# Attention and low-rank feed-forward on one core: the negated row maxima reach DRAM by a transfer of single elements

## The reference, cut to what matters

```python
q = einsum('bsd,dhk->bshk', LN(x), Wq) + bq          # k and v alike
attn = softmax(einsum('bqhd,bkhd->bhqk', q / 8, k), axis=-1)
att = einsum('bqhd,hdm->bqm', einsum('bhqk,bkhd->bqhd', attn, v), Wo) + bo
x = x + LN(att)
x = x + LN(gelu(LN(x) @ U1 @ V1 + b1) @ U2 @ V2 + b2)
```

## Time and profile before

| what | value |
|---|---|
| median of three runs | 2462.3 us (2461.09 to 2462.98) |
| the profiled execution's own time | 2463.04 us |
| its span, first to last instruction | 2461.0 us |
| mean granted TensorE clock | 0.986 |
| busy: PE, ACT, POOL, DVE | 97%, 88%, 84%, 82% |
| the chain that ended last | PE 88%, POOL 8%, DVE 2% |

### The profile page before, as it was taken

One profiled execution on the slowest core, in us unless ns is written; L12 is line 12 of the kernel. 1 busy time (PEld: TensorE's weight loads), 2 busy tenths in 40 slices (PEclk: granted clock), 3 DMA queues, 4 the chain that ended last, 5 costly groups with the idle time before them and its releaser, 6 DMA issues.

```text
span 2461.0 us, 44224 instructions
## 1 busy us (share of the span) xinstructions
PE 2382.9 (97%) x15724; PEld 1183.9 (48%) x15724; DVE 2011.0 (82%) x3148; ACT 2154.1 (88%) x2499; POOL 2071.8 (84%) x1188
## 2 busy tenths in 40 slices
PE   6999999999999999999999999999999999998985
PEld 3455544545545454545445445445545445544432
DVE  6888888888888888888888888888888888886735
ACT  5998999998999999898999999899999998997873
POOL 4888888888888888888888888888888888898985
PEclk8999999999999999999999999999999999999987
DMA  1000001000010000000010000100001000010001
GB/s 50 28 14 27 27 15 32 27 22 19 27 32 15 27 27 19 28 27 27 14 32 27 18 24 27 33 14 27 27 14 32 27 23 26 27 40 18 23 27 35
DMA packets 60773, 63.13 MB, mean 26 GB/s; under 512 B 25900, under 2 KB 44204, under 8 KB 60556
## 3 DMA queue, kind: packets, MB, share of 16 engines
q1 hardware_dynamic: 59548, 59.97, 7.8%
q10 hardware_dynamic: 1008, 0.33, 0.1%
HBM read 57.40 MB, written 2.62 MB: 24 GB/s over the span
## 4 chain that ended last, share of the span: by engine, by line
PE 88%; POOL 8%; DVE 2%; issue 1%; ACT 1%; DMA 0%; POOLq 0%; ACTq 0%; DVEq 0%
PE o_ps L419 34%; PE spare_ps L376 13%; PE score_ps L398 10%; PE score_ps L404 9%; PE score_ps L401 9%; POOL total L1028 5%; PE spare_ps L362 3%; PE spare_ps L344 3%; PE spare_ps L353 2%; PE spare_ps L449 2%; PE spare_ps L431 1%; DVE max_part L815 1%; POOL xn L1055 1%; POOL ln_rstd L1034 1%; PE spare_ps L383 1%
## 5 line engine op out<-in xcount | busy, mean ns | idle before, releaser
L1028 POOL TENSOR_TENSOR total<-total,probs 128x832 f32<-128x832 f32 x896 | 1768.2, 1973 | 294.3 <-ACT probs L638 217.5
L815 DVE TENSOR_REDUCE max_part<-spare_ps 128x1 f32<-128x512 f32 x2027 | 1303.7, 685 | 334.7 <-PE spare_ps L376 320.5
L638 ACT ACTIVATE probs<-score_ps 128x1024 f32<-128x1024 f32 x1024 | 994.0, 1023 | 218.9 <-PE score_ps L404 218.3
L628 ACT ACTIVATE score_ps<-m_all 128x1024 f32<-128x1024 f32 x1024 | 1011.2, 1029 | 5.2 <-DMA m_all<-m_scratch 5.2
L419 PE MATMUL o_ps<-probs,v_sb 128*64 128x512 f32 x4096 | 989.1, 597 | 0.0
L419 PEld LDWEIGHTS o_ps<-probs,v_sb 128*64 128x64 f32 x4096 | 299.8, 137 | 387.9 <-issue 252.6
L376 PE MATMUL spare_ps<-k_hi,q_hi 64*128 64x512 f32 x2027 | 456.6, 446 | 19.5 <-DVE max_part L815 15.6
L398 PE MATMUL score_ps<-q_hi,k_hi 64*128 64x512 f32 x2048 | 426.8, 412 | 7.9 <-ACT score_ps L628 7.9
L404 PE MATMUL score_ps<-q_hi,k_lo 64*128 64x512 f32 x2048 | 406.2, 392 | 0.0
L401 PE MATMUL score_ps<-q_lo,k_hi 64*128 64x512 f32 x2048 | 405.1, 391 | 0.0
L376 PEld LDWEIGHTS spare_ps<-k_hi,q_hi 64*128 64x128 f32 x2027 | 193.4, 184 | 433.4 <-issue 247.1
(11 more groups left out here) (116 smaller groups left out, 979.6 us busy)
## 6 DMA issues: line engine op xcount, KB each, us to landing
m_all<-m_scratch SPq DMA_DIRECT2D x64, 512.0 KB, 3.6
denom<-denom_scratch SPq DMA_DIRECT2D x126, 128.0 KB, 2.8
y_acc<-in_L_attn_x SPq DMA_DIRECT2D x8, 256.0 KB, 6.3
xg<-in_L_attn_x SPq DMA_DIRECT2D x8, 256.0 KB, 4.2
block_out<-z_sb SPq DMA_DIRECT2D x8, 256.0 KB, 2.3
m_scratch<-max_rows SPq DMA_DIRECT2D x64, 4.0 KB
denom_col<-denom SPq DMA_DIRECT2D x63, 4.0 KB
denom_scratch<-denom_col SPq DMA_DIRECT2D x63, 4.0 KB, 1.4
```

Of the source, the lines that this page charges most:

```text
L628: nc.scalar.activation(score_ps[st % 2][:], m_all[:, G % 2], ACT.Copy).then_inc(s["seed_done"], 1)
L638: nc.scalar.activation(probs[:, st % RING], score_ps[st % 2][:], ACT.Exp, scale=SCALE).then_inc(s["exp_done"], 1)
L815: nc.vector.reduce_max(max_part[:, G % 2, h, qt, kc:kc + 1], bank[max_bank(n, h)], AX.X).then_inc(s["max_done"], 1)
L1028: nc.gpsimd.tensor_tensor(others(total[:, G % 2]), so_far, others(probs[:, st % RING]), ALU.add).then_inc(s["sum_done"], 1)
```

## The change

`neg_max` shrinks to its 8 columns (no clearing). The transposition on TensorE, its turn in the spare banks, ScalarE's copy and the tile `max_rows` go, with the semaphores `m_ps` and `m_evac`. SyncE writes `neg_max` itself to `m_scratch`, with the axes exchanged by the access pattern: 128 partitions by 8 elements of 4 bytes, each to a place of its own (the elements of one partition 512 bytes apart). This stands at d = 4 (`sp_m_out`), ahead of the way back of the denominators; the read to `m_all` stays at d = 5 (`sp_m_back`).

```diff
-Q_AT, M_AT = 2, 5
+Q_AT, M_OUT_AT, M_BACK_AT = 2, 4, 5
...
-        if d == M_AT and G + 1 < CHUNKS:
-            use("M", G + 1)
...
-        neg_max = sb("neg_max", [P, 2, HD])
-        max_rows = sb("max_rows", [2 * TC, 2, P])
+        neg_max = sb("neg_max", [P, 2, 2 * TC])
...
-            def transpose_max(self, G, name=None):
-                ps = self.take(name or SPARE["M", G], "M", G)
-                self.pe.wait_ge(s["neg_max_done"], G + 1)
-                nc.tensor.matmul(ps[0:HD, 0:P], neg_max[:, G % 2, :], ident[:], start=True, stop=True).then_inc(s["m_ps"], 1)
...
-        def act_m(act, G, name=None):
-            act.wait_ge(s["m_ps"], G + 1)
-            if G >= 2:
-                act.wait_ge(s["m_out"], 16 * (G - 1))
-            nc.scalar.activation(max_rows[:, G % 2, :], bank[name or SPARE["M", G]][0:2 * TC, 0:P], ACT.Copy).then_inc(s["m_evac"], 1)
...
         def dve_neg_max(dve, G):
             dve.wait_ge(s["max_done"], 2 * T * (G + 1))
-            if G == 0:
-                dve.wait_ge(s["const_ready"], 3)
             if G >= 2:
-                dve.wait_ge(s["m_ps"], G - 1)
-            nc.vector.tensor_reduce(neg_max[:, G % 2, 0:2 * TC], max_part[:, G % 2].rearrange("p h q k -> p (h q) k"), AX.X, ALU.max,
+                dve.wait_ge(s["m_out"], 16 * (G - 1))
+            nc.vector.tensor_reduce(neg_max[:, G % 2, :], max_part[:, G % 2].rearrange("p h q k -> p (h q) k"), AX.X, ALU.max,
                                     negate=True).then_inc(s["neg_max_done"], 1)
...
-            nc.gpsimd.memset(neg_max[:], 0.0).then_inc(s["const_ready"], 1)
...
-        def sp_m(sp, G):
-            sp.wait_ge(s["m_evac"], G + 1)
+        def sp_m_out(sp, G):
+
+            sp.wait_ge(s["neg_max_done"], G + 1)
+            if G >= 2:
+                sp.wait_ge(m_dma[G % 2], 16 * (G // 2))
+            sp.dma_start(m_dram[G % 2].rearrange("r n -> n r"), neg_max[:, G % 2, :],
+                         allow_slow_non_contiguous=True).then_inc(s["m_out"], 16)
+
+        def sp_m_back(sp, G):
             if G >= 2:
                 sp.wait_ge(s["seed_done"], (G - 1) * T)
-            sp.dma_start(m_dram[G % 2], max_rows[:, G % 2, :]).then_inc(s["m_out"], 16)
             sp.wait_ge(s["m_out"], 16 * (G + 1))
             sp.dma_start(m_all[:, G % 2].rearrange("p h n -> p (h n)"),
                          m_dram[G % 2].rearrange("r n -> (r n)").partition_broadcast(P)).then_inc(m_dma[G % 2], 16)
...
                 if d == DENOM_OUT_AT and G:
                     sp_denom_out(sp, G - 1)
+                if d == M_OUT_AT and G + 1 < CHUNKS:
+                    sp_m_out(sp, G + 1)
                 if d == RECIP_AT and G:
                     sp_denom_back(sp, G - 1)
-                if d == M_AT and G + 1 < CHUNKS:
-                    sp_m(sp, G + 1)
+                if d == M_BACK_AT and G + 1 < CHUNKS:
+                    sp_m_back(sp, G + 1)
```

More of the change, by code:

```diff
@@ L238, in build @@
             eps_added minus_mean stats_done mv_done rstd_done xn_done
-            xnT_ps_ready xnT_done first_copied first_split w_in0 w_in1 k_ps q_ps v_ps m_ps k_hi_done q_hi_done k_split q_split v_done
-            m_evac m_out m_dma0 m_dma1 seed_done score_ready exp_done pv_done sum_done part_done merge_done denom_ps_ready
+            xnT_ps_ready xnT_done first_copied first_split w_in0 w_in1 k_ps q_ps v_ps k_hi_done q_hi_done k_split q_split v_done
+            m_out m_dma0 m_dma1 seed_done score_ready exp_done pv_done sum_done part_done merge_done denom_ps_ready
             denom_copied col_dma recip_done scratch_dma denom_dma o_copied o_norm_done wo_ps_ready y_done max_ready max_done
@@ L315, in take @@
                     pe.wait_ge(s["v_done"], k)
-                elif was == "M":
-                    pe.wait_ge(s["m_evac"], k + 1)
                 elif was == "L":
@@ L523, in pe_program @@
                     me.project_v(0, 0, TC, FIRST_V_BANK)
-                if n == T:
-                    me.transpose_max(0, "r2")
             for n in range(DOUBLES):
@@ L541, in pe_program @@
                     me.project_q(G + 2)
-                if d == M_AT and G + 1 < CHUNKS:
-                    me.transpose_max(G + 1)
                 if projected_at(G, d) is not None:
@@ L723, in act_program @@
             act_copy(act, "Q", 1, FIRST_Q_BANK[1])
-            act_m(act, 0, "r2")
             act_seed(act, 0)
@@ L736, in act_program @@
                     act_q(act, G + 2)
-                if d == M_AT and G + 1 < CHUNKS:
-                    act_m(act, G + 1)
                 if n + 1 < DOUBLES:
@@ L1196, in sp_program @@
             sp.dma_start(bo_sb[:], bo.partition_broadcast(P)).then_inc(s["bo_in"], 16)
-            sp_m(sp, 0)
+            sp_m_out(sp, 0)
+            sp_m_back(sp, 0)
             for n in range(DOUBLES):
```

## The result

The changed kernel takes 2767.9 us (median of four runs, 2767.25 to 2776.31) against 2461.7 us: a ratio of 1.1251, interval 1.1229 to 1.1273. It is 306 us slower, where I forecast 7 us faster.

A forecast was written before the change was run, and what follows sets the result against it. TensorE and ScalarE, arriving together, were taken to bound 918 to 2190 us, GpSimd what follows. 59 chunks at 0.125 us save 7.4 us, transfer and prologue nothing: 2462.3 - 7.4 = 2454.9, say 2455 us, range 2449 to 2460.

The forecast's parts named there:

- The bound and the removed work: TensorE and ScalarE bound 918 to 2190 us; dropping transposition and copy saves 0.125 us in 59 chunks, 7.4 us.
- The two distances: At d = 5: maxima to next maxima 2.20 us, not 2.39; first exponential to first seed 1.83, not 1.98.
- The transfer: SyncE's element write of neg_max to DRAM lands 2.4 to 3.2 us after issue, hidden, costed at nothing.
- The cover: Time hiding the element write before the seeds wait: slack grows from 1.0 to 3 us.
- the point from which it decides: Elements may land by 1020.1, 7.4 us after issue; each microsecond later is paid once per chunk.
- The prologue: At the start, elements land at 39.1 to 39.9, the read at 43.0 to 43.8; 1.2 us to spare, no cost.
- The rival of the slow write: Elements one behind another on one engine take 26 us; SyncE holds the read, seeds wait: 3,600 us; chance 0.07.
- both paces of rows 7: Per DMA engine, 18 ns per packet (b1c load) and at most 33 ns (denom_scratch write), used for the element write.
- Its milder form: Element write at 0.12 us per element on each engine: 8.1 us, 0.7 over, 44 us lost, 2506; within chance 0.07.
- The Trainium skill's rule: Plain DMA transposing by strides is 19 times slower than the crossbar; for the 1,024 elements 1.6 us, hidden.

The follow-up runs named there:

- without the landing: Changed kernel with the maxima written as 32-byte runs and seeds read straight on, in the wrong order: 2456.1 us, and once more 2455.7 us.
- the probe: Kernel before plus the changed kernel's 1,024-element DRAM write on SyncE in idle time, waited for: it waits 9.3 us; the run took 2461.0 us.
- own512: Kernel before plus an extra SyncE write of 1,024 elements to DRAM, 512 bytes for each: it waits 2.2 us; the run took 2461.0 us.
- step8: Kernel before plus an extra SyncE write of 1,024 elements to DRAM, 8 bytes apart: it waits 5.4 us; the run took 2461.0 us.
- the read first: Changed kernel with SyncE's read to m_all ahead of the denominators' way back: 2587.2 us, ratio 1.0499.

## Why the prediction was wrong, point by point

**The bound and the removed work: right.** The two distances came out at 2.19 and 1.82 us for 2.20 and 1.83, and without the landing the change is worth 5.8 to 6.9 us for 7.4.

**The transfer: here it failed.** The step reads "as it is the same direction: 1.4 + 56 x 0.033 = 3.2 us from issue to landing", and from it follows "So I cost the transfer at nothing". It took 10.1 us on average (8.8 us in the chunk shown; 9.3 us plus its issue in the probe). I scaled a landing by the pace of packets, and that pace was right. But completion isn't at the end of the packets. Neither row was a bound: `b1c` writes on the chip, where the probe shows single elements to be harmless, and `denom_scratch` puts two runs in 64 bytes, where the probes show that neighbours cost nothing. The thing that the new transfer alone had, 16 writes to every 64 bytes, was in no row, and I took the nearest row for a bound.

**The cover: the point from which it decides was near, the price was not.** The elements had 7.4 us and took 10.1. Behind them came what the step didn't have at all: the denominators' write, sent later on the same queue, is confirmed only after the elements, and SyncE waits for it first. So the read to `m_all` goes out 12.2 us after the elements (mean of 63 chunks) where 7.4 + 1.4 = 8.8 us were allowed, 3.4 us over, and lands in 4.4 us rather than 3.6, for which the cause is open. That makes some 4.2 us; the seeds' stall measures 229 / 61 = 3.8 us per chunk. The price "each microsecond over it is paid once per chunk" leaves out the 1.3 us per chunk behind the stall.

**"The prologue ... so nothing": wrong** for the same reason. Elements issued at 36.0 let the read go at 45.1, and the first seed starts at 49.96 rather than 42.97.

**The rival of the slow write** had the place, the sign and the mechanism of the loss (SyncE holds the read, the next seeds wait), with a chance of 0.07. Its reason was another one, elements at a slow pace. What spoke against it, "both paces of rows 7 are four times and more below", was pace again, and it was wrong by its own figures: 0.11 us is 3.3 times 0.033 us. Its milder form (8.1 us, 2506) came close in the landing and had a seventh of the loss, 44 us.

**The Trainium skill's rule** ("VectorE: DVE Perf Modes", section "The three transpose paths") as I applied it gave 1.6 us, and no row of mine contradicted it; measured it is 10.1 us for the landing. The warning's sign was right for this transfer. My scaling by the number of elements was not: 128 elements wait 7.2 us and 1,024 wait 9.3. The page gives its factor for a large innermost step in the destination, which I left out. Here such a step doesn't decide: `own512`, with 64 KB from one element of a partition to the next, waits 2.2 us, and `step8`, with 8 bytes, 5.4.

## What to carry to other kernels

Before a transfer to DRAM with small runs goes on a tight path, count how many writes it puts to 64 bytes of DRAM: here up to four waited 1.1 to 2.8 us, 8 to 16 waited 3 to 9 us, and the transfer behind them on the queue waited along. Read a landing from the wait behind the transfer, not from its packets. Where columns must become rows, turn them on the chip (here 0.21 us of an idle VectorE) and write long runs; and expect a stall of a TensorE-bound loop to cost more than its length: what was left over beside the waits was 78 us to 229 in the changed kernel and 25 us to 100 with the read first, a quarter to a third.

## What the runs showed of the hardware that was not expected

- 1,024 single 4-byte writes to DRAM are on record within 1.5 us and confirmed 10.1 us after their issue (mean). The wait goes by how densely they lie: for 128 elements 1.1 to 1.3 us at one or two to 64 bytes, 1.7 at four, 3.0 at eight, 7.4 at sixteen.
- Another transfer behind them, to other addresses, is confirmed only after them: 7.7 us after its issue rather than 1.4.
- ScalarE's copy of 1,024 columns from SBUF to PSUM takes 2095 ns with 32 bytes from element to element in the source and 1029 ns without; a weight load of TensorE takes 306 ns with a step of 16 bytes and 184 ns without.
- A stall of 3 us of TensorE was followed by a stretch of 7.6 us at a mean granted clock of 0.78, with 0.50 (1.2 GHz) in 3 us of it.
